# A mixture of experts computed for the chosen experts only: tokens sorted into blocks of 128, with plain fp32 products

## The reference

```python
h2 = rmsnorm(X, norm2_w).reshape(B * S, d)          # layer 0, 8 experts, hidden size 256
probs = softmax(h2 @ router_w); topw, topi = top_k(probs, 2); topw = softmax(topw)
shared = swiglu(h2, sh_gate, sh_up, sh_down)
gate = einsum('td,edf->etf', h2, e_gate);  up = einsum('td,edf->etf', h2, e_up)
eout = einsum('etf,efd->etd', silu(gate) * up, e_down)
X + shared + einsum('etd,te->td', eout, combine)    # combine is zero but for the top two
```

## Time and profile before

| | |
|---|---|
| median of 3 runs | 496.2 us (495.94 to 496.96) |
| span of the profiled execution, first to last instruction | 494.2 us |
| PE busy | 453.3 us, 92% |
| DVE busy | 358.1 us, 72% |
| POOL busy | 319.0 us, 65% |
| ACT busy | 287.7 us, 58% |
| mean granted clock of PE | 0.993 |

### The profile page before, as it was taken

How to read it: one execution, slowest core, us unless ns; L and a number is a source line. 1 busy time by engine, 2 the same in 40 slices (tenths; PEclk the granted TensorE clock), 3 DMA queues, 4 the chain that set the end, 5 groups by cost and what they waited for, 6 DMA issues and landing times.

```text
span 494.2 us, 11017 instructions
## 1 busy us (share of the span) xinstructions
PE 453.3 (92%) x3724; PEld 341.0 (69%) x3724; DVE 358.1 (72%) x930; ACT 287.7 (58%) x559; POOL 319.0 (65%) x525
## 2 busy tenths in 40 slices
PE   6859888999999999999999999899989997899996
PEld 5646555676677777677767877686858775687674
DVE  4657877899988878968656747775766756877864
ACT  2424566766787774565674476536664477446452
POOL 7895889898868676546934584547635573446553
PEclk9988999999999999999999999999999999999999
DMA  6340000040101000020000000000000000000000
GB/s 164 79 140 2 0 3 3 1 119 5 56 3 57 1 1 0 1 55 0 2 1 0 2 1 1 0 0 0 0 0 1 2 1 0 23 1 23 0 23 21
DMA packets 19353, 9.80 MB, mean 20 GB/s; under 512 B 6535, under 2 KB 18792, under 8 KB 19304
## 3 DMA queue, kind: packets, MB, share of 16 engines
q1 hardware_dynamic: 18584, 9.04, 6.9%
q10 hardware_dynamic: 720, 0.13, 0.2%
HBM read 8.12 MB, written 1.05 MB: 19 GB/s over the span
## 4 chain that ended last, share of the span: by engine, by line
PE 49%; POOL 18%; DVE 14%; issue 13%; ACT 4%; POOLq 1%; ACTq 0%; DVEq 0%
PE PS L1774 9%; PE PS L1776 9%; PE PS L1775 8%; POOL HLO L618 3%; DVE work L1382 2%; PE PS L1700 2%; PE PS L1694 2%; PE PS L1930 2%; DVE work L1387 2%; PE PS L1689 2%; PE PS L1662 2%; PE PS L1734 2%; POOL rs L437 1%; DVE RDT L1135 1%; PE PS L1677 1%
## 5 line engine op out<-in xcount | busy, mean ns | idle before, releaser
L618 POOL TENSOR_TENSOR HLO<-work,HHI 128x512 fp32r<-128x512 f32 x111 | 143.1, 1292 | 128.2 <-ACT HHI L869 124.8
L876 ACT ACTIVATE work<-PS 128x512 f32<-128x512 f32 x112 | 66.8, 596 | 91.1 <-PE PS L1776 88.4
L1382 DVE TENSOR_TENSOR work<-work,PS 128x512 f32<-128x512 f32 x104 | 71.0, 683 | 57.3 <-ACT work L876 32.3
L1387 DVE TENSOR_TENSOR work<-PS,work 128x512 f32<-128x512 f32 x112 | 77.2, 691 | 19.2 <-POOL HLO L618 10.8
L869 ACT ACTIVATE HHI<-work 128x512 fp32r<-128x512 f32 x111 | 69.8, 629 | 29.3 <-DVE work L1387 29.1
L1099 DVE TENSOR_REDUCE nmax<-PS 128x4 f32<-128x512 f32 x64 | 42.2, 683 | 8.3 <-PE PS L1662 7.9
L738 ACT ACTIVATE EX<-PS 128x512 f32<-128x512 f32 x64 | 35.0, 603 | 12.3 <-PE PS L1677 12.1
L1774 PE MATMUL PS<-HHI,W0H_down 128*128 128x512 f32 x72 | 35.0, 485 | 0.2
L1774 PE MATMUL PS<-H2H,W0H_gate 128*128 128x512 f32 (+1 forms) x72 | 32.0, 444 | 0.7 <-ACT work L876 0.7
L1930 PE MATMUL PS<-CWT,sel 128*128 128x512 bf16 (+1 forms) x68 | 26.5, 390 | 6.5 <-DVE work L1382 6.0
L1774 PE MATMUL PS<-H2H,W0H_up 128*128 128x512 f32 (+1 forms) x72 | 29.2, 406 | 2.9 <-DVE work L1387 2.9
(11 more groups left out here) (355 smaller groups left out, 1204.3 us busy)
## 6 DMA issues: line engine op xcount, KB each, us to landing
X<-in_x_dram SPq DMA_DIRECT2D x4, 256.0 KB, 5.2
raw<-in_L_ffn_e_gate_dram SPq DMA_DIRECT2D x1, 1024.0 KB, 5.5
raw<-in_L_ffn_e_up_dram SPq DMA_DIRECT2D x1, 1024.0 KB, 7.2
out_dram<-X SPq DMA_DIRECT2D x3, 256.0 KB, 2.3
raw<-in_L_ffn_We_gate_dram SPq DMA_DIRECT2D x1, 512.0 KB, 4.0
raw<-in_L_ffn_We_up_dram SPq DMA_DIRECT2D x1, 512.0 KB, 3.9
raw<-in_L_ffn_We_down_dram SPq DMA_DIRECT2D x1, 512.0 KB, 4.1
ctx_nat<-in_ctx_dram SPq DMA_DIRECT2D x1, 462.0 KB
```

Source lines behind the costliest of these rows:

```text
L618: pool.tensor_tensor(HLO[t][:], HH[k % 2][:], HHI[t][:].bitcast(F32), ALU.subtract).then_inc(m_sem["lo"], 1)
L876: act.activation(SG[c % 2][:], PS[:, c % 2, :], ACT.Silu).then_inc(S["silu"], 1)
L1382: dve.tensor_tensor(SG[c % 2][:], SG[c % 2][:], PS[:, 4, :], ALU.mult).then_inc(S["scaled"], 1)
L1387: dve.tensor_tensor(HH[c % 2][:], PS[:, 2 + c % 2, :], SG[c % 2][:], ALU.mult).then_inc(S["hid"], 1)
```

## The change

The first mixture is computed for the two chosen experts of each token only.

- *Sorting.* The tokens are taken in three sets: `SETS` = group 0, groups 1 and 2, group 3. From the two chosen experts (0/1 tile OH, summed MB) PE counts by products with a triangular matrix (`count_places`), and DVE works out each token's place in blocks of 128 rows that belong to one expert each (`places`, tiles POS and EID). The number of blocks is fixed at the most that can be needed: 15, 23 and 15; places that no token takes hold zeros.
- *Moving.* POOL scatters normalised tokens to XS in device memory by indirect DMA (one for each tile of 128 tokens and choice), SP loads the blocks to XB, and stores the results YB to YS; POOL gathers them by indirect DMA (GY), and DVE adds them with the tokens' weights (`of_first_expert`, `of_second_expert`).
- *Units.* A unit is 128 tokens for one expert: 16 units of the shared expert straight from the tokens, 53 blocks. Gate and up are one plain fp32 product of 512 columns with the tokens as the stationary side; two transposes turn the hidden tile, two plain fp32 products of 128 columns go down. There is no splitting of these weights or hidden tiles any more, and no spreading of weights. The experts' numbers are loaded into PE's registers from EID, and the weights addressed by them.
- *Order.* The loop on the chip is written out; the woven steps stand at times in us (`MATCH_AT`, `placed`, `matched`), turned into a unit or chunk number by 1.55 us per unit and 2.3 us per chunk; no step of group g may stand behind chunk 10g - 1.

```diff
-            for k, n in enumerate(KINDS):
-                r = raw[k % 2]
-                if k == 2:
-                    sp.wait_ge(halved, 1)
...
+SETS = ((0, 1), (1, 3), (3, 4))
+UNIT_US, CHUNK_US = 1.55, 2.3
+MATCH_AT = (44.0, 88.0, 117.5, 147.0)
...
+        def slot_of(g, us):
+            return min(slot_at(MATCH_AT[g] + us), NU + NCH1 * g - 1)
...
+            def blocks_in(i):
+                s, _, first, n = QUADS[OF_EXPERTS[i]]
+                sp.wait_ge(xs_in[s], 16 * TOP * len(tiles_of(s)))
+                if i >= NXB:
+                    sp.wait_ge(u_sem["t1"], OF_EXPERTS[i - NXB] + 1)
...
+            def scatter(s):
...
+                for i, b in enumerate(tiles_of(s)):
+                    for k in range(TOP):
+                        pool.indirect_dma_start(out=XS[s][:], out_offset=bass.IndirectOffsetOnAxis(ap=POS[s][:, k, i:i + 1], axis=0),
+                                                in_=HN[b // GB][:, b % GB, :], in_offset=None).then_inc(xs_in[s], 16)
...
+                return matched(g, (1.0, lambda: root(0, "sc")), (12.0, bias), (31.0, lambda: root(GB, "sc2")), (41.0, low_tokens))
...
+            steps = by_slot(placed((2.0, lambda: token_scales(3)), (10.0, lambda: scatter(1)), (35.0, lambda: gather(0)),
+                                   (43.0, lambda: scatter(2)), (80.0, lambda: gather(1)), (84.0, lambda: gather(2)), (111.0, lambda: gather(3)))
...
+                return matched(g, (0.0, lambda: of_first_expert(g)), (1.6, lambda: of_second_expert(g)), (13.5, mx), (14.9, bmax), (18.0, soft),
+                               (21.2, bcol), (23.0, product), (24.0, weights), (29.0, update), (42.0, route_a), (42.6, route_b),
+                               (45.0, route_c), (46.0, route_d))
...
+            def load_experts(q):
+                s, _, first, n = QUADS[q]
+                if s is not None:
+                    pe.wait_ge(r_sem["pos"], 2 * s + 2)
+                    for j in range(n):
+                        experts[BEGIN[q] + j] = pe.value_load(EID[s][0:1, first + j:first + j + 1], min_val=0, max_val=E0 - 1)
...
+                pe.matmul(PS[:, u % 2, :], XF[q % NXH][:, x], weights_of(u, W0G, 2 * F0, 0, 2 * F0), start=True, stop=True).then_inc(u_sem["gu"], 1)
...
+                y = PS[:, Y_BANK[q % 2], j * D:(j + 1) * D]
+                for c in range(2):
+                    ins = pe.matmul(y, HTU[u % 2][:, c * P:(c + 1) * P], weights_of(u, W0D, 2 * D, c * D, D), start=(c == 0), stop=(c == 1))
...
+                for u, (q, j) in enumerate(UNITS):
+                    gate_up(u)
+                    if j == 1 and q + 1 < NQ:
+                        turn_unit_tokens(q + 1)
+                        load_experts(q + 1)
+                    if u >= 1:
+                        turn_hidden(u - 1)
+                    if u >= 2:
+                        down0(u - 2)
+                    for f in inserts.get(u, ()):
+                        f()
...
+                return matched(g, (9.0, t), (12.0, sims), (14.3, bts), (19.0, ats), (20.5, bbts), (20.6, hqs), (22.5, hcs), (26.0, outs),
+                               (38.0 - 0.8, turned), (41.0, scored), (48.8, ct))
```

More of the change, by code:

```diff
@@ L95, in build @@
         work = [sb(f"work{k}", [P, GT]) for k in range(6)]
+        HN = [work[g][:].rearrange("p (b d) -> p b d", b=GB) for g in range(G)]
+        SGU, HMU = ([work[k][:, u * F0:(u + 1) * F0] for u in range(2)] for k in (4, 5))
+        XB = sb("XB", [P, NXB * QUAD * D])
         gstats = sb("gstats", [P, 2 * GB, 6])
@@ new lines, in build @@
+        x_sem = {n: sem(f"x_{n}") for n in ("z", "both")}
+        r1_sem = stage("r1", pe="t lg ct", act="h ht ct_sb", dve="lg_sb cs", pool="low")
+        two = sem("two")
+        m_sem = stage("m", pe="bc g u down yn", act="silu hi yt", dve="scaled hid x", pool="lo")
+        c_sem = stage("c", pe="t s bt at bbt hq hc o", act="xn e3 xt exp at_sb hq_sb",
+                      dve="mx a bc xh xu mv mv2", pool="xb sc sc2")
+        ln_chain = sem("ln_chain")
+        block = ctx.enter_context(nc.Block())
@@ L299, in col, with gy_of, stored @@
             return ap.rearrange("(n a) -> n a", a=1)
+        def gy_of(b):
+            return b % NGY
+        def stored(s):
+            done = sum(1 for q in OF_EXPERTS if QUADS[q][0] <= s)
+            return [16 * len(range(k, done, NYB)) for k in range(NYB)]
         @block.sync
@@ L965, in _ @@
+            units(steps)
+            for g in range(G):
+                chunks(g, steps)
+            last = G * NCH1 - 1
+            act.wait_ge(S["hid"], last + 2)
+            act.wait_ge(S["down"], last - LAG + 2)
+            act.activation(HHI[last % LAG][:], HH[last % 2][:], ACT.Copy).then_inc(S["hi"], 1)
+            act.wait_ge(S["down"], last + 2)
+            act.wait_ge(S["yn"], G)
             for k in range(2):
@@ L2036, in _ @@
+            units(steps)
+            for g in range(G):
+                chunks(g, steps)
+            for k in range(G * NCH1 - LAG, G * NCH1):
+                down(k)
+            pe.wait_ge(S["x"], G)
             for k in range(2):
-                pe.wait_ge(S["yt"], 2 * G + 1 + k)
+                pe.wait_ge(S["yt"], G + 1 + k)
                 for j in range(2):
```

1377 lines of the change are left out of this document (714 added, 663 removed).

## The result

The changed kernel took 569.1 us (median of 4 runs, 565.45 to 571.46) against 496.1 us for the kernel before (495.59 to 496.96): a ratio of 1.146, 95% interval 1.142 to 1.150. The forecast was 506 us, range 468 to 530. The profiled execution took 565.5 us, its span is 563.5 us; the forecast's span was 504. One thing must be known to read the experiments: the same changed kernel took 567.4 us in a second job and 594.7 and 594.2 us in two others, while the kernel before stayed at 496 to 497 us in all of them. Each experiment is therefore set against the changed kernel at the level that its own trace shows.

What follows compares the result with a forecast made beforehand. TensorE's order of work was taken to set the time: attention 168, units 159, second mixture 168 and tail 8.7 gave a 504 us span, plus 2 us made 506 us, against 496.2 before; range 468 to 530.

Steps and rivals of the forecast that it cites:

- saving in products: First mixture on PE: 69 units take 109 us against 166.3 us for 72 chunks, saving 57 us.
- pitch: PE's time from unit to unit where nothing is woven in: 1.58 us; over 1.9 would refute the cost.
- three gaps ahead of chunk groups 2, 3 and 4: Sign on PE in the second mixture: gaps of 10, 18 and 15 us, ended by DVE's last weight piece.
- Squeezed ends: Second mixture, ahead of chunk groups: exposed latency from output products to weights, 10, 18 and 15 us, sum 43.
- The rival that they are covered: Second mixture: latency runs beside PE's own lateness, 43 us falls to 15, total 478 us; chance 0.2.
- First blocks late: Start of units: PE waits 8 us for the first scattered and reloaded tokens; 2 or 19 at the bounds.
- Gather of group 1: Late units: DVE asks at unit 56, before store, eight gathers and landing are done; costs 3 us.
- Register loads: PE's queue ahead of 14 quads: 53 loads of experts' numbers with clamps, 0.6 us exposed per quad, 8 us.
- my cover of 1.2 us: Ahead of each quad: issued products in PE's queue, 0.87 + 0.36 us, hide that much of the register loads.
- the 17 us that I drew from it: Register loads by the skill's 600 ns floor: four take 2.4 us, 1.2 us exposed, 17 us for 14 quads.
- Matching: PE work woven in, about 14 us a group: 21 us among the units, 35 us in the second mixture.
- my sorting term: Units: blocks of routing 2 to 3 us long on DVE exceed its 1.4 us free per unit, costing 4 us.

Runs made afterwards that it cites:

- PE kept busy: Changed kernel with unread fp32 products filling eight long PE waits: 585.2 us, 9 us less than the changed kernel at its level.
- the moves on POOL: Changed kernel with a group's second root ahead of the next group's first, and group 2's gathers later: 574.8 us, 19.9 us less.
- the experiment gave 8.2 there: Changed kernel with each group's second root ahead of the next group's first root on POOL: 579.9 us, 14.6 us less.
- paced scatters: Changed kernel with POOL waiting behind each scatter of set 1 until it has landed: 7.4 us more than the changed kernel's 567.4 us.

## Why the prediction was wrong, step by step

- **Direction and place right.** The saving in products was as worked out: pitch 1.52 us for 1.58. The three gaps ahead of chunk groups 2, 3 and 4 are there, ended by DVE's last weight piece.
- **No term for the clock: the step that was missing.** I took the full level of the earlier trace rows as a property of the kernel. It is that of a PE without long waits: behind the ones seen here (6.1 to 12.3 us) the rows after show 0.57 to 0.79. The estimate from the windows is 32 us (9.7 + 22.2). PE kept busy won back 9 by itself and 4.6 beside the moves on POOL, with a fill that was too long in places. That the rest of the slow products lies beside latencies that end the waits anyway is my reading, and not shown.
- **Squeezed ends, 58 us for 43.** Group 1: (11.0 + 4.7 + 9.9) less three chunks, 18.7 for 10; group 2: 22.3 for 18; group 3: 17.5 for 15. The rival that they are covered is refuted. I had priced the root that stands behind the next group's for group 2 at 8 us; the experiment gave 8.2 there, and 5 more for group 1, where I had not looked for it in POOL's order. Some 0.7 to 1.4 us per end is the first chunk behind it, at the lower clock (with PE kept busy 4.1, 2.6 and 2.3 us in place of 4.9, 3.3 and 3.7).
- **First blocks late, 8 us, became 13 with the loads** (units 1 to 2 take 14.4 us for 1.5). A scatter cost POOL 1.26 us, I had 1.0; the reload took 2.75, I had 2.3; the places came 3 us later; the 1.93 us of loads came on top. But this step was also wrong in kind: with the wait filled by another quad nothing was won in the end. That set 1's blocks and the transfers behind them set the time there is likely from PE's longer wait for them, but part of the loss lies among the stops.
- **Gather of group 1, 3 us, became 8** (9.7 us for 1.5 at unit 59). I priced its chain and not what follows a DVE wait: the hidden product stands behind it in DVE's queue. That the gathers of group 2 stand right behind, 10 us of POOL ahead of group 0's tokens, had no step.
- **Register loads, 8 us: right in size by luck** (6.6 measured). Four loads take 2.9 us where PE's queue has waited, 183.6 to 186.5 us, 0.7 us each with their clamps, and I had 0.45; with my cover of 1.2 us that would have been 24 us for 14 quads. Most quads hide them, so two errors cancel. The Trainium skill, "DMA: Bandwidth & Descriptors" (Latency and other measured facts), gives 600 ns as a floor of a tensor load; the trace agrees with it. It doesn't agree with the 17 us that I drew from it, since the cover in the queue is larger than I had counted.
- **Attention, 8 us that I had excluded.** I wrote that it gains nothing, and gave a loss no term. In before the mixture's early products filled PE's gaps at its end; after, PE waits 2.4 us there, the clock is 0.66 from 165 to 175 us, and the first gate product stands at 175.07. That the missing products are the cause is argued, not tested.
- **Matching and sorting, too cheap.** Among the chunks 45 us are left for the matching's 35 (194.0 less 90.1 less 58.5), and some 40 with PE kept busy. Among the units, PE's waits for DVE at the hidden turn (17.1 us) hold, besides the gather's 6.5, eight stalls of 0.5 to 2.7 us, 10.6 in sum; my sorting term had 4 us.
- **What ended the forecast's range:** 468 to 530 left out that several of these come together. Eight, 26 and 26 us over in the three stages are one tendency: each new wait was priced by its own length, and not by what stands behind the waiting instruction and by the clock after it. In the terms of the sum: squeezed ends 43 to 58 us, first blocks 8 to 13, gather 3 to 8, stalls behind DVE 4 to 10.6, attention 0 to 8, and the clock, with no term, 9 us by the experiment. These overlap, since the lower clock lies in all of them.

The Trainium skill, "Perfetto Trace Analysis" (DMA Instruction, SWDGE), says that for such a transfer the profiler's end is the end of the writing of descriptors and not that of the data. The trace agrees. The eighth scatter on POOL:
```profile
178.26 1.06 POOL L666 DMA_INDIRECT XS<-work,POS  x1 [0.30 <-issue]
```
It ends there at 179.32 and lands at 180.59, 1.27 us later. My bound of 0.2 to 2.3 us from the earlier trace rows mixed the two: some 1.26 us for each of the eight are POOL's, and only 1.27 us of the last landing come on top.

## What to carry to other kernels

Sparse work that saves an engine's time turns its waits into the bound, so price the order of every in-order queue, at each place where two groups meet: here one exchange of two roots on POOL, 0.9 us in a plan of times, was worth 14.6 us. When a kernel that never let TensorE stand still gets waits of 6 us, put a term for the lower clock into the sum, estimated from the slowed work behind the waits; here the estimate was 32 us, and filling the waits won back 9. And an indirect transfer has three prices: POOL's own time, the landing, and, at times, stops of other engines beside it.

## What the hardware showed that was not expected

- While POOL issued indirect transfers, and just behind them, ScalarE and VectorE stood still though what they waited for was done, ScalarE for 4.3 and 5.7 us at the two places shown. It showed in all nine traces of three jobs with indirect scatters and gathers, in a tenth only where the gathers are, and in neither trace with plain transfers of the same size; the changed kernel's traces in the two other jobs are free of it, and so is that with paced scatters. It costs the units some 22 us (207.3 and 208.2 us against 184.6 and 185.7). Neither the cause nor whether a single transfer does it is settled.
- Not all that parts the two levels is the stops. The first silu of the units comes at 182.9 and 183.1 us in the slower traces, but at 180.9 with plain transfers too, which have no stops, and at 176.1 in the first trace. From 70 to 80 us the granted clock is 0.67 to 0.69 in those three and 1.00 in the first trace; from 60 to 70 us PE was busy 6.8 us in each.
- An indirect transfer of 128 rows of 512 bytes took POOL 0.96 us plus 0.30 to the next, whether scatter or gather; a plain one of the same size on the same queue 0.55 us.
- In before the granted clock stayed full from 50 us on with PE idle for 8% of the span in small pieces. After, it fell behind the single long waits, but at the attention's end too (0.66 from 165 to 175 us), where PE had waited no more than 2.4 us at a time.
